# Cross attention with folded weights: another order of the opening work on one NeuronCore

## The chip, the cores and the metric

The program runs on one core of one Trainium2 chip. The metric is the device time of one execution in microseconds (us). The kernel before took 1906.45 us, the median of 3 runs (1904.95 to 1910.61).

## What is computed

The model has two layers of three blocks each. The change touches only the first block of the first layer, a cross attention from 4 x 256 tokens of width 256 to a context of 4096 tokens, with a mask and a single head of width 1024:

```python
x = x + _L0_xattn_ref(_layernorm(x), ctx_1024, ctx_1024, mask, Wq, bq, Wk, bk, Wv, bv, Wo, bo)
...
Q = q @ Wq.T + bq
K = k @ Wk.T + bk
V = v @ Wv.T + bv
e = jnp.einsum('bsd,btd->bst', Q, K) / jnp.sqrt(jnp.float32(d_k))
e = jnp.where(mask == 0, MASK_FILL, e)
a = jax.nn.softmax(e, axis=-1)
y = jnp.einsum('bst,btd->bsd', a, V)
return y @ Wo.T + bo
```

Behind it come a selective scan, a soft mixture of experts, a 16-head cross attention to the same context, a causal attention and a quantised MLP. They are the same in both kernels.

## The kernel before

The block (`cross_attention_wide`, lines 163 to 573) never forms Q, K or V. It folds the weights: A = Wq'Wk (256 x 256) and M = Wv'Wo, so that a score is a token times A times a context column. The biases leave three small things: the column `cq` (Wk'bq, added to the folded queries), the column `u` (Wq'bk, times a token it gives one number of a row) and the number `beta` (bq.bk). From `u` and `beta` comes `small`, and from that `fill`, the value that a masked score gets in each of the 8 query tiles of 128 tokens.

The context arrives transposed, batch by batch (4 batches, two query tiles each), in 8 chunks of 512 columns, 512 KB each. Each chunk is split into two fp32r words: the high word is a cast (line 450, on VectorE, written DVE), the low word is the difference (line 557, on GpSimd, written POOL). A product of two such pairs takes three matmuls per 128 rows (line 156). Both words of every chunk are also stored to memory as `ctx_words` for the second layer, 1 MB per chunk in two transfers (line 220), which SyncE (SP) issues.

The queries are folded in two halves of 512 tokens (line 347), copied out of PSUM by ScalarE (ACT) with `cq` added (line 422) and split into words by VectorE (lines 530 and 532). Then come the tiles. For tile i ScalarE fills a row of scores with the value for masked ones (line 430); TensorE (PE) makes the scores of 8 chunks; VectorE copies the unmasked ones over the filled row (line 458; it counts `kept`) and takes peaks (line 460). ScalarE forms the exponentials in 4 pieces (line 396). In the next turn TensorE transposes them (line 290) and multiplies by the untransposed context, called rows (line 324), while the scores of the tile after are already made. `weighted(i)` is that second part; in it, for each even tile, VectorE also splits the chunks of the next batch. M and the constant row `rowC` (lines 269, 371, 545, 548) are made between the scores of tile 0 and those of tile 1, and tile 1's fill waits for `rowC`.

No planner sets the order. Each engine has one function (`wide_sp`, `wide_pe`, `wide_act`, `wide_dve`, `wide_pool`) and runs it from top to bottom; semaphores tie them together. SP's function is the order in which the transfers enter the queue. Its loop issues the mask of tile i+1 (line 224, 2 MB, one buffer) once tile i's scores are all kept, and around an odd tile the first four chunks of the next batch:

```python
        if i + 1 < NT:
            sp.wait_ge(s.kept, CH * (i + 1))
            load_mask(i + 1)
```

The next batch's chunks use four buffers, so chunks 4 to 7 are loaded one by one behind the stores of chunks 0 to 3. VectorE may overwrite the words of a batch only when all its stores have landed (`split_high` waits for `stored`).

The four weights share memory with the scores: Wq and Wk lie in the scores' first buffer, Wv and Wo in the second.

Of the kernel before, what the change touches and what calls it, by code (L numbers as in the profile page):

```python
# [9 lines left out]
I32 = mybir.dt.int32  # L10
# [151 lines left out]
XW_DH, XW_MASKED, XW_PIECES, XW_RAW = 1024, -2.0 ** 15, 4, 4  # L162
XW_HK = XW_DH // P
# [3 lines left out]
def wide_tiles(k, scope):  # L167
    def sb(name, shape, dt=F32):
# [12 lines left out]
    t["mask"], t["E"] = sb("mask", [P, S2], I32), sb("scores", [P, 2, S2])  # L181
    t["wq"], t["wk"], t["wv"], t["wo"] = (
        t["E"][:, n // 2, n % 2 * HK * D:(n % 2 + 1) * HK * D].rearrange("p (k d) -> p k d", k=HK) for n in range(4))
# [20 lines left out]
def wide_sp(k, t, s, ctxT_in, ctxN_in):  # L204
# [21 lines left out]
    for n in ("Wq", "Wk"):  # L226
        sp.dma_start(t["w" + n[1]], d["L0_xattn_" + n].rearrange("(k p) d -> p k d", p=P)).then_inc(s.wqk, 16)
    load_mask(0)
    for c in range(CH):
        load_words(0, c)  # L230
    for n, name in (("wv", "L0_xattn_Wv"), ("wo", "L0_xattn_WoT")):
        sp.dma_start(t[n], d[name].rearrange("(k p) d -> p k d", p=P)).then_inc(s.wvo, 16)
    for c in range(CH):
        store_words(0, c)
        load_rows(0, c)
    for i in range(NT):
        b = i // QT
# [11 lines left out]
        if i == 0:  # L249
            continue  # L250
# [12 lines left out]
def wide_pe(k, t, s, ctxT_in, ctxN_in):  # L263
    pe, PS, HK = k.pe, k.PS, XW_HK

    def folded(left, right):
        for c in range(KD):
            for h in range(HK):
                last = pe.matmul(PS[:, 4, c * D:(c + 1) * D], left[:, h, c * P:(c + 1) * P], right[:, h, :],
                                 start=(h == 0), stop=(h == HK - 1))  # L270
        return last
# [56 lines left out]
    yt_pe(k, 0, 0)  # L328
    pe.wait_ge(s.wqk, 32)
    folded(t["wq"], t["wk"]).then_inc(s.a_pe, 1)  # L330
    pe.wait_ge(s.biases, 48)
    pe.wait_ge(s.bias_dot, 2)
    for c in range(KD):
        for col, left, right in ((c, t["wk"], t["bq"]), (KD + c, t["wq"], t["bk"])):
            for h in range(HK):
                pe.matmul(PS[:, 5, col:col + 1], left[:, h, c * P:(c + 1) * P], right[:, h:h + 1],
                          start=(h == 0), stop=(h == HK - 1))
    pe.matmul(PS[:, 5, 4:5], k.ones[:], t["dot"][:], start=True, stop=True).then_inc(s.vec_pe, 1)

    pe.wait_ge(s.a, 1)  # L340
    for half in range(TOK // BANK):
        wait_yt(k, pe, 0, half + 1)
        for c in range(KD):
            if half:
                pe.wait_ge(s.q_raw, KD * (half - 1) + c + 1)
            for kd in range(KD):
                last = pe.matmul(PS[:, 6 + c, :], t["A"][:, kd, c * P:(c + 1) * P],
                                 k.YT[:, kd, half * BANK:(half + 1) * BANK], start=(kd == 0), stop=(kd == KD - 1))
            last.then_inc(s.q_pe, 1)
    pe.wait_ge(s.vec, 1)  # L350
# [6 lines left out]
    pe.wait_ge(s.q_lo, 4)  # L357
    for i in range(NT):
        for c in range(CH):
# [3 lines left out]
        if i:  # L363
            weighted(i - 1)
            continue
        pe.wait_ge(s.wvo, 32)
        folded(t["wv"], t["wo"]).then_inc(s.m_pe, 1)
# [13 lines left out]
def wide_act(k, t, s, ctxT_in, ctxN_in):  # L381
# [34 lines left out]
    act.wait_ge(s.vec, 1)  # L416
    for half in range(TOK // BANK):
        for c in range(KD):
            act.wait_ge(s.q_pe, KD * half + c + 1)
            if half:  # L420
                act.wait_ge(s.q_lo, KD * (half - 1) + c + 1)
            act.activation(t["q_raw"][:, c, :], PS[:, 6 + c, :], ACT.Identity, bias=t["cq"][:, c:c + 1],
                           scale=XW_SCALE).then_inc(s.q_raw, 1)
    act.wait_ge(s.small, 2)
    for i in range(NT):
        if i == 1:
            act.wait_ge(s.row, 1)
        if i >= 2:
            act.wait_ge(s.turned, CH * (i - 1))
        act.activation(t["E"][:, i % 2, :], k.zero[:, 0:1].to_broadcast([P, S2]), ACT.Identity,  # L430
                       bias=t["fill"][:, i:i + 1]).then_inc(s.filled, 1)
# [10 lines left out]
def wide_dve(k, t, s, ctxT_in, ctxN_in):  # L442
# [8 lines left out]

    def scores(i):
        dve.wait_ge(s.filled, i + 1)
# [2807 lines left out]
```

## Time and profile before

| | us |
|---|---|
| median of 3 runs | 1906.45 |
| lowest, highest | 1904.95, 1910.61 |
| the profiled execution's own time | 1893.33 |
| its span in the profile | 1891.5 |
| PE busy in it | 1751.8 (93%) |
| DVE busy in it | 1453.6 (77%) |
| ACT busy in it | 1164.5 (62%) |
| mean granted TensorE clock, share of full | 0.969 |

Times in the rows are microseconds from the span's start. L450 is line 450 of the kernel before. "PE" is TensorE's matmuls, "DVE" VectorE, "ACT" ScalarE, "POOL" GpSimd, "SPq" SyncE's issuing of transfers. A matmul of float32 operands shows as two records, so that 16 matmuls stand as x32. The names `xw_scores` on lines 269 and 336 stand for the weights, which lie in that buffer.

### The profile page before, as it was taken

The page shows a single profiled execution, that of the slowest core. Times are in us where ns is not written, and L with a number is a line of the kernel's source. Part 1 is how long each engine was busy: PE and PEld are TensorE (multiplying, and loading weights), DVE is VectorE, ACT ScalarE, POOL GpSimd, SP SyncE. Part 2 cuts the span into 40 slices and gives each one's busy share as a digit, 9 for nine tenths or more (in the row PEclk, how much of TensorE's full clock was granted, in tenths as well). Part 3 has the DMA queues.
Part 4 walks back from the last instruction along what each step waited for, and adds up shares of the span by engine and source line. Part 5 has one row for each costly group of instructions (what it writes and reads, how often), then busy time and mean ns, then how long its engine had stood idle before and what let it go on. Part 6 is the DMA issues. An engine that isn't in the chain of part 4 may idle for free. (4 is left out here: it accounts for less than half of the span.)

```text
span 1891.5 us, 32678 instructions
## 1 busy us (share of the span) xinstructions
PE 1751.8 (93%) x12516; PEld 1202.2 (64%) x12516; DVE 1453.6 (77%) x1664; ACT 1164.5 (62%) x2100; POOL 398.9 (21%) x267
## 2 busy tenths in 40 slices
PE   6989989989999998999988999999999999999875
PEld 5877877457766776878776555555555555555534
DVE  7546643577899886676764899999999999998565
ACT  0333332577777765353541588888888988888363
POOL 4134120145445532232212000010010000000041
PEclk8999999999999999999998899999999999999897
DMA  9798780248866881222225746655566555630000
GB/s 357 271 349 324 276 315 0 95 141 299 317 244 238 304 286 46 69 73 70 73 37 113 173 95 118 123 107 112 103 119 118 107 97 120 116 66 20 1 0 22
DMA packets 171816, 279.79 MB, mean 148 GB/s; under 512 B 21855, under 2 KB 100479, under 8 KB 164495
## 3 DMA queue, kind: packets, MB, share of 16 engines
q1 hardware_dynamic: 170366, 277.52, 51.6%
q8 instruction: 101, 1.65, 0.4%
q10 hardware_dynamic: 1296, 0.19, 0.1%
q14 instruction: 53, 0.43, 0.1%
HBM read 187.07 MB, written 88.14 MB: 146 GB/s over the span
## 5 line engine op out<-in xcount | busy, mean ns | idle before, releaser
L2414 DVE TENSOR_REDUCE xn_peaks<-psum 128x2 f32<-128x1024 f32 x512 | 622.4, 1224 | 41.6 <-PE psum L2212 33.5
L2369 ACT ACTIVATE moe_mix_transposed<-psum 128x512 f32<-128x512 f32 x1024 | 552.6, 597 | 67.6 <-PE psum L2217 34.1
L2217 PE MATMUL psum<-xn_q_stack,xn_k_words 50*128 50x256 f32 x2048 | 374.9, 305 | 6.5 <-DVE xn_peaks L2414 4.0
L2217 PEld LDWEIGHTS psum<-xn_q_stack,xn_k_words 50*128 50x128 f32 x2048 | 248.1, 185 | 206.1 <-ACT moe_mix_transposed L2369 183.4
L2212 PE MATMUL psum<-xn_k_words,xn_q_stack 50*128 50x512 f32 x1024 | 372.4, 452 | 4.6 <-DMA xn_q_stack<-q_rows 3.1
L2249 PE MATMUL psum<-moe_mix_transposed,xn_v 128*32 128x256 f32 x4096 | 327.0, 391 | 2.0 <-issue 0.3
L934 POOL TENSOR_TENSOR mx_state<-mx_du,mx_b_all_channels 128x1024 f32<-128x1024 f32 x64 | 154.0, 2406 | 196.3 <-ACT mx_b_all_channels L1116 83.7
L2212 PEld LDWEIGHTS psum<-xn_k_words,xn_q_stack 50*128 50x128 f32 x1024 | 185.2, 186 | 13.6 <-issue 8.2
L1197 DVE TENSOR_TENSOR_SCAN mx_state<-psum,mx_state 128x1024 f32<-128x1024 f32 x64 | 146.2, 2285 | 50.3 <-ACT psum L1126 42.7
L324 PE MATMUL psum<-xw_ctx_natural,xw_weights_transposed 128*128 128x256 f32 x512 | 124.1, 388 | 12.3 <-DVE xw_weights_transposed L476 12.0
L2249 PEld LDWEIGHTS psum<-moe_mix_transposed,xn_v 128*32 128x32 f32 x4096 | 81.6, 108 | 73.8 <-issue 7.3
L2042 POOL CAST xn_neg_words<-xn_neg_max 128x4 fp32r<-128x4 f32 x32 | 6.1, 190 | 548.3 <-DVE xn_neg_max L2421 548.3
L731 ACT ACTIVATE ctx_k_words<-psum,ctx_bk 128x512 fp32r<-128x512 f32 x128 | 85.5, 690 | 53.5 <-PE psum L156 47.6
L156 PE MATMUL psum<-ctx_wv_words,ctx_chunk_words 128*128 128x256 f32 x768 | 114.6, 299 | 0.6 <-ACT ctx_k_words L731 0.3
L156 PEld LDWEIGHTS psum<-ctx_wv_words,ctx_chunk_words 128*128 128x128 f32 x768 | 101.5, 192 | 17.0 <-issue 12.2
L324 PEld LDWEIGHTS psum<-xw_ctx_natural,xw_weights_transposed 128*128 128x128 f32 x512 | 94.6, 193 | 26.9 <-DVE xw_weights_transposed L476 15.4
L156 PE MATMUL psum<-ctx_chunk_words,ctx_wk_words 128*128 128x512 f32 x384 | 108.0, 423 | 1.5 <-DMA ctx_chunk_words<-ctx_words 1.1
L156 PE MATMUL psum<-moe_w_words,moe_hidden_words 128*128 128x256 f32 x768 | 101.7, 292 | 5.2 <-issue 5.2
L156 PE MATMUL psum<-xw_ctx_transposed_words,xw_q_folded_words 128*128 128x512 f32 x384 | 99.2, 413 | 5.6 <-DVE xw_scores L458 5.0
L156 PE MATMUL psum<-moe_slot_input_words,moe_w_words 128*128 128x512 f32 x384 | 92.7, 395 | 10.7 <-ACT moe_hidden L1581 8.9
L156 PEld LDWEIGHTS psum<-moe_w_words,moe_hidden_words 128*128 128x128 f32 x768 | 95.9, 195 | 9.7 <-issue 8.9
L1206 DVE TENSOR_TENSOR mx_state<-mx_state,mx_c_all_channels 128x1024 f32<-128x1024 f32 x64 | 97.2, 1519 | 0.0
(354 smaller groups left out, 2573.8 us busy)
## 6 DMA issues: line engine op xcount, KB each, us to landing
xn_k_words<-k_words SPq DMA_DIRECT2D x384, 128.0 KB, 6.6
ctx_words<-xw_ctx_transposed_words SPq DMA_DIRECT2D x64, 512.0 KB
ctx_chunk_words<-ctx_words SPq DMA_DIRECT2D x64, 512.0 KB, 5.5
k_words<-ctx_k_words SPq DMA_DIRECT2D x128, 256.0 KB, 2.5
v_all<-ctx_v SPq DMA_DIRECT2D x32, 544.0 KB, 3.2
xn_v<-v_all SPq DMA_DIRECT2D x32, 544.0 KB, 5.1
xw_mask<-in_mask_BxSxS_ik SPq DMA_DIRECT2D x8, 2048.0 KB, 8.2
xw_ctx_natural<-in_ctx SPq DMA_DIRECT2D x32, 512.0 KB, 6.8
```

The costliest lines, as they stand in the source:

```text
L156: last = k.pe.matmul(out, l, r, start=(n == 0), stop=(n == len(terms) - 1))
L324: last = pe.matmul(PS[:, 5, 0:D], t["ET"][:, c % 2, j, :], t["ctxN"][:, c, j, :], start=(c + j == 0), stop=(c == CH - 1 and j == JC - 1))
L731: act.activation(t["keys"][:, m, n, :], k.PS[:, bank("keys", i, m), :], ACT.Identity, bias=t["bk"][:, m:m + 1]).then_inc(kr[m], 1)
L934: pool.tensor_tensor(t["state"][:, i % MX_STATES, :, :], t["du"][:, m % 2, None, :].to_broadcast([P, MX_NQ, MX_HALF]), t["Bb"][:, q * MX_N ...
L1197: dve.tensor_tensor_scan(flat, t["decay"][i % MX_DECAYS].rearrange("p n t -> p (n t)"), flat, 0.0, ALU.mult, ALU.add).then_inc(s.scan, 1)
L1206: dve.tensor_tensor(h, h, t["Cb"][:, q * MX_NQ:(q + 1) * MX_NQ, :], ALU.mult).then_inc(s.cmul, 1)
L2042: pool.tensor_copy(t["neg_words"][:, :, :, XN_SHIFT], neg).then_inc(s.words, 1)
L2212: return pe.matmul(PS[:, 2 * (x % 2) + a, :], Q[narrow_rows(a), m // XN_PAIRS % 2, m % XN_PAIRS, q * P:(q + 1) * P], K[m % XN_KSLOTS][narr ...
L2217: return pe.matmul(PS[:, narrow_bank("exp", n, step, a), half * S:(half + 1) * S], K[n % XN_KSLOTS][narrow_rows(a), kt * P:(kt + 1) * P], ...
L2249: last = pe.matmul(PS[W * j:W * (j + 1), XN_ACC, 0:S], t["V"][:, n % 2, at:at + W], t["weights"][:, step % 4, a, half, :], start=(step == ...
L2369: act.activation(t["weights"][:, step % 4, a, :, :], bank.rearrange("p (t s) -> p t s", t=2), ACT.Exp, scale=XN_SCALE).then_inc(s.taken, 1)
L2414: dve.tensor_reduce(t["peaks"][:, m % 2, q, :, c], PS[:, 2 * (x % 2):2 * (x % 2) + 2, :], AX.X, ALU.max).then_inc(s.top_read, 1)
```

## The change

It changes the opening of the block on each engine.

- The bias `bk` is copied into a 257th column of Wk's tile, so that the fold that makes A gives `u` as its 257th column. `cq` is made as a row, bq'Wk (8 matmuls with a single stationary column and 256 moving ones, into one partition), copied to memory and turned into a column by two matmuls against a one. The 33 matmuls with one moving column of lines 336 and 338 become 2 + 1.
- Batch 0's high words are made by ScalarE (`first_high`), its low words by VectorE (`first_low`). Six high words come ahead of the first half of the queries and two behind; the low words are spread over VectorE's opening. GpSimd has no part in batch 0's words.
- The second half of the queries moves behind the scores of tile 0, on TensorE, ScalarE and VectorE.
- The fills of tiles 0 and 1 are cut into 4 pieces of 1024, and each chunk of scores waits for its own piece.
- `bvB` (8 instructions on VectorE) moves from the opening to behind tile 0's scores.
- SP loads Wk ahead of Wq, the words of batch 0 ahead of the first mask, all rows of batch 0 behind Wv and Wo with no stores between them, and tile 1's mask ahead of the stores. The 16 stores of batch 0 stand behind that mask, and so ahead of batch 1's first chunks.

The core of the diff:

```diff
-    for n in ("Wq", "Wk"):
-        sp.dma_start(t["w" + n[1]], d["L0_xattn_" + n].rearrange("(k p) d -> p k d", p=P)).then_inc(s.wqk, 16)
-    load_mask(0)
+    for n in ("Wk", "Wq"):
+        sp.dma_start(t["w" + n[1]][:, :, 0:D], d["L0_xattn_" + n].rearrange("(k p) d -> p k d", p=P)).then_inc(s.wqk, 16)
     for c in range(CH):
         load_words(0, c)
+    load_mask(0)
...
     for c in range(CH):
-        store_words(0, c)
+        sp.wait_ge(s.ctx_hi, c + 1)
+        sp.wait_ge(s.ctx_lo, c + 1)
         load_rows(0, c)
...
                 if b == 0:
                     sp.wait_ge(s.small, 1)
+                    sp.wait_ge(s.q_pe, 2 * KD)
...
             load_mask(i + 1)
         if i == 0:
+            for c in range(CH):
+                store_words(0, c)
             continue
```

```diff
@@ wide_pe
+    for h in range(HK):
+        last = pe.matmul(PS[0:1, 0, 0:D], t["bq"][:, h:h + 1], t["wk"][:, h, 0:D], start=(h == 0), stop=(h == HK - 1))
+    last.then_inc(s.vec_pe, 1)
+    pe.wait_ge(s.bias_dot, 1)
+    folded(t["wq"], t["wk"], [PS[:, 4 + c, 0:D + 1] for c in range(KD)]).then_inc(s.a_pe, 1)
...
     for c in range(KD):
-        for col, left, right in ((c, t["wk"], t["bq"]), (KD + c, t["wq"], t["bk"])):
-            for h in range(HK):
-                pe.matmul(PS[:, 5, col:col + 1], left[:, h, c * P:(c + 1) * P], right[:, h:h + 1],
-                          start=(h == 0), stop=(h == HK - 1))
+        pe.matmul(PS[:, 1, c:c + 1], t["z"][0:1, c * P:(c + 1) * P], k.ones[0:1, 0:1], start=True, stop=True)
...
     pe.wait_ge(s.a, 1)
+    queries(0)
+    pe.wait_ge(s.vec, 2)
     for q in range(NT):
...
-    pe.wait_ge(s.q_lo, 4)
+    pe.wait_ge(s.q_lo, KD)
...
+        queries(1)
         pe.wait_ge(s.wvo, 32)
```

```diff
@@ wide_act
+    for c in range(XW_SOON):
+        first_high(c)
+    act.wait_ge(s.vec, 2)
+    queries(0)
+    for c in range(XW_SOON, CH):
+        first_high(c)
...
+        pieces = XW_PIECES if i < XW_BY_PIECES else 1
+        for piece in range(pieces):
...
+        if i == 0:
+            queries(1)
@@ wide_dve
+    dve.tensor_copy(t["wk"][:, :, D], t["bk"][:]).then_inc(s.bias_dot, 1)
...
-    for c in range(CH):
-        split_high(0, c)
...
+    first_low(0)
+    first_low(1)
...
+    dve.tensor_copy(t["z"][0:1, :], PS[0:1, 0, 0:D]).then_inc(s.vec, 1)
+    for c in range(2, XW_SOON - 1):
+        first_low(c)
@@ wide_pool
-    for c in range(CH):
-        split_low(0, c)
```

The order of SP's transfers at the block's opening, before (`xw_ctx_natural<-in_ctxT` are batch 0's words, `<-in_ctx` the rows, `ctx_words` the stores; the pair of stores and rows comes eight times, two of them shown):

```order
L224 DMA xw_mask<-in_mask_BxSxS_ik 128x4096
L208 DMA xw_ctx_natural<-in_ctxT 128x2x512 x8
L232 DMA xw_scores<-in_L_xattn_Wv 128x8x256
L232 DMA xw_scores<-in_L_xattn_WoT 128x8x256
L220 DMA ctx_words<-xw_ctx_transposed_words 128x2x512 x2
L212 DMA xw_ctx_natural<-in_ctx 128x4x256
```

and of the change:

```order
L211 DMA xw_ctx_natural<-in_ctxT 128x2x512 x8
L227 DMA xw_mask<-in_mask_BxSxS_ik 128x4096
L235 DMA xw_scores<-in_L_xattn_Wv 128x8x256
L235 DMA xw_scores<-in_L_xattn_WoT 128x8x256
L215 DMA xw_ctx_natural<-in_ctx 128x4x256 x8
L227 DMA xw_mask<-in_mask_BxSxS_ik 128x4096
L223 DMA ctx_words<-xw_ctx_transposed_words 128x2x512 x16
L211 DMA y_normed<-in_ctxT 128x2x512 x2
L211 DMA y_transposed<-in_ctxT 128x2x512 x2
L227 DMA xw_mask<-in_mask_BxSxS_ik 128x4096
```

The 16 stores of batch 0 now stand between tile 1's mask and batch 1's first four chunks; from tile 2's mask on the order is the old one.

VectorE's opening before, from the copy of A on:

```order
L518 COPY xw_a<-psum 128x512
L450 CAST xw_ctx_transposed_words<-xw_ctx_natural 128x1024 x8
L522 TENSOR_SCALAR xw_cq<-psum 128x2
L523 COPY xw_u<-psum 128x2
L524 COPY xw_bq_dot_bk<-psum 128x1
L530 CAST xw_q_folded_words<-xw_q_folded 128x512
L532 TENSOR_TENSOR xw_q_folded_words<-xw_q_folded,xw_q_folded_words 128x512
```

and of the change, from the small bias products on:

```order
L485 TENSOR_TENSOR xw_ctx_transposed_words<-xw_ctx_natural,xw_ctx_transposed_words 128x1024 x2
L567 COPY xw_z<-psum 1x256
L485 TENSOR_TENSOR xw_ctx_transposed_words<-xw_ctx_natural,xw_ctx_transposed_words 128x1024 x3
L571 COPY xw_a<-psum 128x512
L572 COPY xw_u<-psum 128x2
L574 TENSOR_SCALAR xw_cq<-psum 128x2
L575 COPY xw_bq_dot_bk<-psum 128x1
L485 TENSOR_TENSOR xw_ctx_transposed_words<-xw_ctx_natural,xw_ctx_transposed_words 128x1024
L493 CAST xw_q_folded_words<-xw_q_folded 128x512
```

The eight casts that stood between A and `cq` are gone; five low words now lie ahead of A, in VectorE's wait for the fold, and one behind `cq`.

## Rows read from the trace of the kernel before

**Rows 1.** The page's busy line, and the chain of waits asked for 0 to 130 us

```profile
PE 1751.8 (93%) x12516; PEld 1202.2 (64%) x12516; DVE 1453.6 (77%) x1664; ACT 1164.5 (62%) x2100; POOL 398.9 (21%) x267
0 pieces in order of time: start us, us, what
```

**Rows 2.** Timeline of TensorE, 14 to 76 us: start, duration, what, [idle before it]

```profile
14.85 7.59 PE L269 MATMUL psum<-xw_scores 128*128 128x256 f32 x32
28.86 3.55 PE L336 MATMUL psum<-xw_bk,xw_scores 128*128 128x1 f32 x16
...
32.70 5.50 PE L347 MATMUL psum<-y_transposed,xw_a 128*128 128x512 f32 x8
...
47.15 4.20 PE L353 MATMUL psum<-xw_u,y_transposed 128*128 128x1 f32 x32
51.21 13.96 PE L156 MATMUL psum<-xw_ctx_transposed_words,xw_q_folded_words 128*128 128x512 f32 x48
65.00 7.07 PE L269 MATMUL psum<-xw_scores 128*128 128x256 f32 x32
71.91 3.62 PE L371 MATMUL psum<-xw_scores,xw_bv_all_columns 128*128 128x256 f32 x16
```

**Rows 3.** Timeline of VectorE, 22 to 56 us

```profile
22.48 0.69 DVE L518 COPY xw_a<-psum 128x512 f32<-128x512 f32 x1 [5.70 <-PE psum L269]
23.09 17.79 DVE L450 CAST xw_ctx_transposed_words<-xw_ctx_natural 128x1024 fp32r<-128x1024 f32 x8
40.80 0.15 DVE L522 TENSOR_SCALAR xw_cq<-psum 128x2 f32<-128x2 f32 x1
...
43.40 2.72 DVE L532 TENSOR_TENSOR xw_q_folded_words<-xw_q_folded,xw_q_folded_words 128x512 fp32r<-128x512 f32 x1
...
46.48 0.69 DVE L532 TENSOR_TENSOR xw_q_folded_words<-xw_q_folded,xw_q_folded_words 128x512 fp32r<-128x512 f32 x1
...
55.59 0.73 DVE L458 COPY_PREDICATED xw_scores<-xw_mask,psum 128x512 f32<-128x512 int32 x1 [3.77 <-ACT xw_scores L430]
```

**Rows 4.** Timeline of ScalarE, 41 to 56 us

```profile
41.11 1.26 ACT L422 ACTIVATE xw_q_folded<-psum,xw_cq 128x512 f32<-128x512 f32 x2 [25.43 <-DVE xw_bq_dot_bk L524]
...
51.85 3.71 ACT L430 ACTIVATE xw_scores<-zero,xw_fill 128x4096 f32<-128x4096 f32 x1 [3.81 <-DVE xw_fill L537]
```

**Rows 5.** Issues of 3 to 4 and of 6.6 to 6.8 us: KB, us to landing

```profile
xw_mask<-in_mask_BxSxS_ik SPq DMA_DIRECT2D x1, 2048.0 KB, 15.9
...
xw_ctx_natural<-in_ctxT SPq DMA_DIRECT2D x1, 512.0 KB, 13.9
```

**Rows 6.** Busy time by stretch: PE, PEld, DVE, ACT, POOL, granted clock, DMA share, GB/s

```profile
20.00:26.00 6.00, 6.00 (x47) 5.72 (x45) 3.52 (x4) 0.00 (x0) 2.08 (x1) 1.00 1.05 388
26.00:32.00 6.00, 6.00 (x31) 6.00 (x31) 6.00 (x3) 0.00 (x0) 6.00 (x3) 0.51 1.07 366
...
50.00:57.00 7.00, 7.00 (x21) 5.76 (x22) 1.77 (x5) 4.99 (x2) 0.00 (x0) 0.51 1.06 400
57.00:65.00 8.00, 8.00 (x36) 6.47 (x35) 7.79 (x13) 0.00 (x0) 0.00 (x0) 1.00 1.06 399
...
79.00:90.00 11.00, 10.94 (x52) 8.64 (x51) 9.98 (x15) 1.33 (x2) 2.67 (x4) 1.00 0.00 0
```

**Rows 7.** Timeline of SP's issuing, 65 to 110 us

```profile
65.97 0.35 SPq L224 DMA_DIRECT2D xw_mask<-in_mask_BxSxS_ik  x1
...
90.12 0.34 SPq L224 DMA_DIRECT2D xw_mask<-in_mask_BxSxS_ik  x1
94.95 0.88 SPq L220 DMA_DIRECT2D ctx_words<-xw_ctx_transposed_words  x2
...
107.50 1.51 SPq L208 DMA_DIRECT2D y_transposed<-in_ctxT  x1
```

**Rows 8.** Timeline of VectorE, 102 to 178 us, its splits of batches 1 and 2

```profile
102.64 0.75 DVE L450 CAST xw_ctx_transposed_words<-y_normed 128x1024 fp32r<-128x1024 f32 x1 [3.68 <-DMA ctx_words<-xw_ctx_transposed_words]
...
114.69 0.69 DVE L450 CAST xw_ctx_transposed_words<-y_transposed 128x1024 fp32r<-128x1024 f32 x1 [3.33 <-DMA ctx_words<-xw_ctx_transposed_words]
...
178.31 0.69 DVE L450 CAST xw_ctx_transposed_words<-y_transposed 128x1024 fp32r<-128x1024 f32 x1 [3.06 <-DMA y_transposed<-in_ctxT]
```

**Rows 9.** Busy time of 156 to 158 us, columns as in rows 6

```profile
156.00:158.00 2.00, 2.00 (x13) 1.74 (x13) 1.93 (x4) 0.00 (x0) 0.00 (x0) 1.00 0.00 0
```

More of the change, by code:

```diff
@@ L264, in wide_pe, with folded, queries @@
     pe, PS, HK = k.pe, k.PS, XW_HK
-    def folded(left, right):
-        for c in range(KD):
-            for h in range(HK):
-                last = pe.matmul(PS[:, 4, c * D:(c + 1) * D], left[:, h, c * P:(c + 1) * P], right[:, h, :],
-                                 start=(h == 0), stop=(h == HK - 1))
-        return last
+    def folded(left, right, outs):
+        for c, out in enumerate(outs):
+            for h in range(HK):
+                last = pe.matmul(out, left[:, h, c * P:(c + 1) * P], right[:, h, :], start=(h == 0), stop=(h == HK - 1))
+        return last
+    def queries(half):
+        wait_yt(k, pe, 0, half + 1)
+        for c in range(KD):
+            if half:
+                pe.wait_ge(s.q_raw, KD * (half - 1) + c + 1)
+            for kd in range(KD):
+                last = pe.matmul(PS[:, 6 + c, :], t["A"][:, kd, c * P:(c + 1) * P],
+                                 k.YT[:, kd, half * BANK:(half + 1) * BANK], start=(kd == 0), stop=(kd == KD - 1))
+            last.then_inc(s.q_pe, 1)
     def scores(i, c):
@@ L365, in wide_pe @@
             continue
+        queries(1)
         pe.wait_ge(s.wvo, 32)
-        folded(t["wv"], t["wo"]).then_inc(s.m_pe, 1)
+        folded(t["wv"], t["wo"], [PS[:, 4, c * D:(c + 1) * D] for c in range(KD)]).then_inc(s.m_pe, 1)
         pe.wait_ge(s.small, 1)
@@ L415, in wide_act, with first_high, queries @@
     yt_act(k, 0)
-    act.wait_ge(s.vec, 1)
-    for half in range(TOK // BANK):
+    def first_high(c):
+        act.wait_ge(ctxT_in[c], 16)
+        act.copy(t["ctxT"][:, c, 0, :, :], t["raw"](0, c)).then_inc(s.ctx_hi, 1)
+    def queries(half):
         for c in range(KD):
@@ L429, in wide_act @@
             act.wait_ge(s.turned, CH * (i - 1))
-        act.activation(t["E"][:, i % 2, :], k.zero[:, 0:1].to_broadcast([P, S2]), ACT.Identity,
-                       bias=t["fill"][:, i:i + 1]).then_inc(s.filled, 1)
+        pieces = XW_PIECES if i < XW_BY_PIECES else 1
+        for piece in range(pieces):
+            width = S2 // pieces
+            act.activation(t["E"][:, i % 2, piece * width:(piece + 1) * width], k.zero[:, 0:1].to_broadcast([P, width]),
+                           ACT.Identity, bias=t["fill"][:, i:i + 1]).then_inc(s.filled, 1)
+        if i == 0:
+            queries(1)
         if i:
@@ L537, in wide_dve @@
     dve.tensor_scalar(t["fill"][:], t["small"][:], XW_MASKED, None, ALU.add).then_inc(s.small, 1)
+    for c in range(XW_SOON + 1, CH):
+        first_low(c)
     for i in range(NT):
@@ L543, in wide_dve @@
         row_peak(0)
+        queries(1)
+        for h in range(HK):
+            last = dve.tensor_scalar(t["bvB"][:, h, :], k.ones[:], t["bv"][:, h:h + 1], None, ALU.mult)
+        last.then_inc(s.wide, 1)
         dve.wait_ge(s.m_pe, 1)
```

80 lines of the change are left out of this document (42 added, 38 removed).

## The prediction

> **What bounds the kernel now.** The busy line puts TensorE at 93% of the span, but that is an average over six blocks, and the chain of waits says nothing of this one: asked for the first 130 us it has no piece there [rows 1]. So I read the first 180 us engine by engine in the timelines, and then the transfers.
>
> TensorE first [rows 2]: fold of A until 22.4, bias products until 32.4, first half of the queries until 38.2, then a wait for the queries to be copied out, the `u` products from 47.15, and tile 0's scores only from 51.2. Who held it back is VectorE [rows 3]: between A (ready at 23.2) and `cq` (40.8) stand eight casts of context words, 17.8 us of them, and ScalarE waited 25.4 us for `cq` and its two neighbours [rows 4]. Then ScalarE fills a whole row, 3.7 us, before VectorE keeps its first score at 55.6 [rows 3, 4]. When the last chunk is kept, SP issues tile 1's mask: that is the mark of tile 0's end, 65.97 [rows 7]. Tile 1's end is the next mask, at 90.12.
>
> Behind that the bound is another one. From 90 on VectorE waits for transfers at each split, and splits batch 1's last chunk at 114.69 [rows 8]. Tile 2's scores need it. The transfer engines had nothing to do from 79 to 90 [rows 6], then 8 MB in a row: tile 2's mask (2), stores of chunks 0 to 3 (4), chunks 4 to 7 (2). The last of these is issued at 107.50 [rows 7]. So whatever is gained in front counts only as far as that last chunk lands earlier.
>
> **The change, part by part.** Times are those of the profiled execution (its own time 1893.33, which is 13.1 us under the median of the runs; I take the difference of the kernels from the trace and put it on the median).
>
> *Biases and A.* On TensorE bq'Wk comes ahead of the fold: 8 matmuls of 256 columns, 16 records at 7.59/32 = 0.24 us, 3.8 us [rows 2]. No row has a matmul with one stationary column; the bounds are 1.9 us (half, if it ran as a shorter one) and 7.6 us (at half clock), and I take 3.8, since the moving side is that of line 269. The fold starts at 18.7 in place of 14.85 and ends near 26.5; its 257th column is 16 columns more in 4096, below 0.1 us. VectorE copies A (0.7), `u`, `cq`, `beta` (0.15 each), with three small matmuls between: `cq` is there at about 27.9 instead of 41.0. The low words that precede it lie in VectorE's wait for the fold. Cover gone: if words come late. Batch 0's first chunk was issued at 6.7 and landed at 20.6, behind a mask of 2 MB that landed at 19.3 [rows 5]; with that mask behind the words it comes about 2.1 MB / 0.39 = 5.4 us earlier, near 15.4, the next ones 1.3 us apart. ScalarE casts each in about 1.0 us (a quarter of the 3.7 of a row of 4096 [rows 4], though that reads a constant; between 0.9 and 1.3), VectorE subtracts in 1.2 us (twice 0.69 less the fixed part [rows 3]). Five are done by about 24, 2.5 us ahead of the fold.
>
> *GpSimd left out.* The same subtraction took 2.72 us beside GpSimd and 0.69 without it [rows 3]. VectorE's opening now has 8 x 1.2 us without a neighbour where it had 17.8. This is inside the 13 us above, not on top.
>
> *Queries.* The first half takes 5.5 us in a stretch where the granted clock was about 0.5 after the one-column products (26 to 32 us: 0.51, the lower of its two levels, 1.2 GHz [rows 6]). These products are gone, so I take full clock, 3.4 us, with 5.5 as the other end. It runs from 27.5 to 31; the copy and split of it (0.7 + 0.4 + 0.7, twice, staggered) end by 33 behind the `u` products. Those start at 31 and take 4.2 us [rows 2]: TensorE is ready for tile 0 at 35.2, where it was at 51.2. The second half no longer stands in front; it follows tile 0's scores.
>
> *Tile 0.* From the end of the `u` products to the next mask the old kernel took 65.97 - 51.21 = 14.8 us. The clock falls in it as before (0.51 from 50 to 57, behind the `u` products [rows 6]), so I keep this duration. The fill in pieces lets VectorE begin about 2 us sooner than 4.4 us behind TensorE, but TensorE at half clock is then what it waits for: worth 0.3 us, at most 1. Tile 1's mask is issued at 35.2 + 14.5 = 49.7, **16.3 us earlier**. The first mask, now behind the words, lands near 30, seven us before its first use: nothing. Wv and Wo, and the rows, go through the queue with no stores between and are there by 45: nothing.
>
> *Tile 1.* From TensorE's end of tile 0 (48.7): second half 3.6 (3.4 and a start), M 7.1, row 3.6 [rows 2], constant row 0.5, one piece of the fill 1.0, then 10.4 for eight chunks (55.59 to 65.97 [rows 3, 7]): kept by 74.9 where it was 90.1, **15.2 us earlier**. ScalarE's exponentials wait for the second half of the queries, some 5 us later against tile 0's scores; they end near 60, before the fill that waits for the row at 64. VectorE's `bvB` lies in its wait for M: nothing.
>
> *The stores.* 16 transfers, 8 MB, leave the opening, where the queue ran on beside the engines' work, and go behind tile 1's mask. What stands behind them in SP's queue are batch 1's chunks 0 to 3, and behind these tile 2's mask. From 49.7 on the queue must carry 12 MB (mask 2, stores 8, chunks 2) and then the same 8 MB as before, for which the old kernel took 114.69 - 90.12 = 24.6 us. 12 MB are 12.6 million bytes, at the 399 to 400 GB/s of the mixed stretch from 50 to 65 us [rows 6] 31.5 us. Sum: 49.7 + 31.5 + 24.6 = 105.8 for the split that stood at 114.69. VectorE's own path (15.2 us earlier) is ahead of that, and tile 2's mask (issued about 75) is in the queue before the chunks have drained at 81, so no hole opens. The gain is **8.9 us**, and 15.2 - 8.9 = 6.3 us of what was won in front turn into VectorE's waits for transfers between 75 and 106.
>
> On the path that sets the end: the rate of these 20 MB. A rule speaks against the rate that I use. The Trainium skill, DMA: Bandwidth & Descriptors, Specifications, gives a limit of about 358 GB/s between HBM and one core; the trace does not agree, with 400 GB/s over 7 us [rows 6]. By that limit the 20 MB would take 58.6 us in place of 52.4, an estimate that would cut the gain to 2.7.
>
> *Behind it.* Before batch 2 the queue is empty again (156 to 158: 0 GB/s [rows 9]), and its splits wait for transfers as those of batch 1 did, e.g. at 178.31 [rows 8]. That pattern starts from the tiles, so the shift is carried to the block's end and through the five blocks behind, whose code is the same.
>
> So 1893.3 - 8.9 = 1884.4 for a profiled execution, and 1906.45 - 8.9 = **1897.5** for the median. A difference under 0.3% (5.7 us) can't be told from none here.
>
> **Rivals.**
> - *The transfers don't bind (gain 15.2, 1891.3).* The old wait at 102.64 could be one for stores of batch 1 or its order alone. Then the last chunk would have to land at 99.5: 21.0 million bytes in 49.8 us, 421 GB/s with no time to start or to land. Against it stand 400 GB/s with the engines' share above 1 [rows 6]. Chance 0.12.
> - *The long run of transfers is slower (gain 4.0, 1902.5).* Eight MB of stores without loads between is a mix that no row shows. The slowest full stretch in the rows is 366 GB/s, from 26 to 32 us, when stores had joined the loads [rows 6]; at that rate 20 MB take 57.3 us in place of 52.4, and the gain is 8.9 - 4.9. Against it: stores and loads together ran at 400 from 50 to 57. Chance 0.07. The Trainium skill's limit, named above, would send the kernel this way.
> - *The front wins less (gain 1 to 5, about 1903).* If TensorE's clock falls on bq'Wk, the fold takes up to 7.6 us longer, and 8.9 shrinks to 1.3; if the words come 2.6 us later than worked out, the low words delay A by as much. For: the clock did fall after the one-column products [rows 2, 6]. Against: those stream one column per load, these 256, as line 269 does at clock 1.00. Chance 0.12.
> - *Slower, by the stores' new place.* 12 MB now lie between tile 0's end and tile 2's mask; the old kernel had 24.2 us there, and they need 31.5. Where tile 0 ends less than 7.4 us earlier, batch 1's last chunk lands later than before; with a front that wins nothing the time is 1906.45 + 7.4 = 1913.9. It decides at 7.4 us, and I expect 16.3. For it only the price is sure. Chance 0.06, with what makes it more than 5.7 us slower under half of that; the rest of the slower side is a waiting order on SP that I have not seen.
>
> **How the numbers follow.** Forecast 0.63, rivals 0.12, 0.07, 0.12, 0.06. The predicted time is that of the forecast, 1897.5; its own bounds are 1894 (rate 415 GB/s, or a front 2 us better) and 1902 (half clock for the queries and 385 GB/s). Down to 1889 the range takes in the first rival with 2 to 3 us of scatter, up to 1907 the third. Faster by over 0.3% means a gain of 5.7 or more: most of the forecast (0.60 of 0.63) and the first rival, and a part of the third, 0.76; within 0.3% 0.18; slower 0.06.
>
> **What would show it.** The eight casts gone from between A and `cq`; `cq` near 28; TensorE's tile 0 from 35; SP's second mask near 50, the third near 76; transfers without a gap from 50 to about 106 at 395 to 405 GB/s; VectorE's last split of batch 1 near 106, with waits for transfers of some 6 us more in all than before; from there to the end the same distances. I am wrong if the last split of batch 1 shifts by another amount than the end of the span, if the granted clock is 0.5 in the fold, or if the transfers of 50 to 80 us run below 380 GB/s.

## The result, and the profile after

| | before | after |
|---|---|---|
| median of the first 3 runs, us | 1906.45 | 1889.98 |
| lowest, highest | 1904.95, 1910.61 | 1888.43, 1891.06 |
| the profiled execution's own time | 1893.33 | 1889.98 |
| its span | 1891.5 | 1888.1 |
| mean granted clock | 0.969 | 0.970 |

The recorded ratio of these runs is 0.9895 (95% interval 0.9849 to 0.9941); the two medians by themselves give 0.9914, 16.5 us, where 8.9 were forecast. The profiled execution of the kernel before was not one of its three timed runs, that of the change was, and the two profiled spans differ by 3.4 us. So the first question is how much the change is worth at all; two further timings of the unedited change (e1 and e12 below) put it at 7.2 us, and the profile says where they come from. Means, intervals and counts below leave out as slow three executions more than 1.5% above the fastest of their kernel: 1920.9 and 1923.4 of the kernel before, and 1909.5 of e5.

The timeline of TensorE after the change, from 14 to 63 us, answers to [rows 2] (start, duration, what):

```profile
14.84 4.06 PE L349 MATMUL psum<-xw_scores,xw_bq 128*1 128x256 f32 x16
18.83 7.22 PE L276 MATMUL psum<-xw_scores 128*128 128x257 f32 x32
...
26.84 3.70 PE L285 MATMUL psum<-y_transposed,xw_a 128*128 128x512 f32 x8
30.38 4.57 PE L365 MATMUL psum<-xw_u,y_transposed 128*128 128x1 f32 x32
34.81 13.64 PE L156 MATMUL psum<-xw_ctx_transposed_words,xw_q_folded_words 128*128 128x512 f32 x48
48.29 3.60 PE L285 MATMUL psum<-y_transposed,xw_a 128*128 128x512 f32 x8
51.72 7.07 PE L276 MATMUL psum<-xw_scores 128*128 128x256 f32 x32
58.63 3.62 PE L386 MATMUL psum<-xw_scores,xw_bv_all_columns 128*128 128x256 f32 x16
```

The row of bq'Wk takes 4.1 us, the fold ends at 26.05, the first half of the queries runs at full clock (3.7 us, no longer 5.5), and tile 0 begins at 34.8 in place of 51.2.

VectorE's timeline, which answers to [rows 3] and, in its last line, to [rows 8]:

```profile
16.51 2.36 DVE L485 TENSOR_TENSOR xw_ctx_transposed_words<-xw_ctx_natural,xw_ctx_transposed_words 128x1024 fp32r<-128x1024 f32 x2 [1.38 <-ACT xw_ctx_transposed_words L434]
...
19.28 3.47 DVE L485 TENSOR_TENSOR xw_ctx_transposed_words<-xw_ctx_natural,xw_ctx_transposed_words 128x1024 fp32r<-128x1024 f32 x3
26.10 0.69 DVE L571 COPY xw_a<-psum 128x512 f32<-128x512 f32 x1 [3.34 <-PE psum L276]
...
26.94 0.16 DVE L574 TENSOR_SCALAR xw_cq<-psum 128x2 f32<-128x2 f32 x1
...
81.66 0.69 DVE L481 CAST xw_ctx_transposed_words<-y_normed 128x1024 fp32r<-128x1024 f32 x1 [4.81 <-DMA y_normed<-in_ctxT]
...
107.84 0.69 DVE L481 CAST xw_ctx_transposed_words<-y_transposed 128x1024 fp32r<-128x1024 f32 x1 [3.46 <-DMA y_transposed<-in_ctxT]
```

Two low words take 2.36 us; VectorE still waits 3.3 us for the fold, so they cost nothing. `cq` stands at 26.94, 13.9 us earlier. Then the picture turns: the first split of batch 1 waits 4.8 us for its chunk, and the last one is at 107.84, where it was at 114.69. That is 6.85 us gained of 16.65 at tile 1's mask, which SP's timeline shows ([rows 7]):

```profile
49.32 0.34 SPq L227 DMA_DIRECT2D xw_mask<-in_mask_BxSxS_ik  x1
49.75 20.43 SPq L223 DMA_DIRECT2D ctx_words<-xw_ctx_transposed_words  x16
70.27 2.59 SPq L211 DMA_DIRECT2D y_normed<-in_ctxT  x2
...
75.99 1.70 SPq L227 DMA_DIRECT2D xw_mask<-in_mask_BxSxS_ik  x1
```

What the transfer engines did, from busy time by stretch (PE, PEld, DVE, ACT, POOL, granted clock, DMA share, GB/s), answers to [rows 6]:

```profile
42.00:44.00 2.00, 2.00 (x10) 1.64 (x9) 1.93 (x4) 0.00 (x0) 0.00 (x0) 1.00 1.10 348
44.00:47.00 3.00, 3.00 (x15) 2.40 (x14) 2.93 (x5) 0.00 (x0) 0.00 (x0) 1.00 0.82 263
47.00:49.00 2.00, 2.00 (x9) 1.40 (x8) 1.97 (x4) 0.00 (x0) 0.00 (x0) 1.00 0.03 9
49.00:50.00 1.00, 1.00 (x3) 0.38 (x2) 0.96 (x2) 0.00 (x0) 0.00 (x0) 1.00 0.00 0
50.00:55.00 5.00, 5.00 (x21) 3.65 (x20) 3.61 (x13) 3.73 (x5) 0.00 (x0) 1.00 1.01 338
55.00:60.00 5.00, 5.00 (x25) 4.41 (x24) 1.06 (x3) 3.56 (x8) 0.00 (x0) 1.00 0.92 328
60.00:65.00 5.00, 4.44 (x20) 3.44 (x19) 0.83 (x2) 2.26 (x3) 2.14 (x4) 1.00 1.05 407
65.00:70.00 5.00, 5.00 (x23) 4.04 (x22) 4.86 (x8) 2.01 (x2) 3.48 (x5) 1.00 1.05 404
```

They stand still from 47 to 50, then work until the last split without standing still again. The new hole in front and the closed one at 79 to 90 are the same thing: work that was hidden beside the opening has become a stream behind tile 0.

### The profile page after: what moved, and what is told of

Read it like the earlier page. It is cut to its first block and busy times, and to the rows that moved or that the text cites. A ratio compares the mean times of both kernels' runs of the same rounds, so it can differ in the third digit from the quotient of the medians.

```text
span 1888.1 us, 32668 instructions
## 1 busy us (share of the span) xinstructions
PE 1746.3 (92%) x12472; PEld 1195.3 (63%) x12472; DVE 1442.5 (76%) x1666; ACT 1173.5 (62%) x2114; POOL 377.9 (20%) x259
```

## The experiments

Each was timed in turn with the kernel before on one chip: e1, e3, e4 and e5 on the first, e6 to e9 on the second, e10 to e12 on the third. "Last split" is VectorE's split of batch 1's chunk 7 in the profiled execution, "mask" SP's issue of tile 1's mask.

| kernel | ratio to before | 95% interval | mask | last split |
|---|---|---|---|---|
| before | | | 65.97 | 114.69 |
| the change, first profile | 0.9895 | 0.9849 to 0.9941 | 49.32 | 107.84 |
| e1, the change | 0.9955 | 0.9936 to 0.9975 | 45.37 | 104.00 |
| e12, the change | 0.9976 | 0.9948 to 1.0004 | 49.18 | 106.51 |
| e4, only the stores moved | 1.0066 | 1.0034 to 1.0099 | 65.89 | 124.17 |
| e3, stores back | 0.9968 | 0.9945 to 0.9991 | 58.78 | 108.43 |
| e5, half the stores first | 0.9930 | 0.9905 to 0.9955 | 48.98 | 101.86 |
| e10, the same | 0.9953 | 0.9923 to 0.9983 | 49.80 | 102.72 |
| e11, the same with u as a row | 0.9947 | 0.9921 to 0.9972 | 48.93 | 101.72 |
| e6, low words by GpSimd | 0.9967 | 0.9940 to 0.9994 | 46.74 | 104.44 |
| e7, one-column products | 1.0015 | 0.9985 to 1.0045 | 57.51 | 115.84 |
| e8, fills in one piece | 0.9970 | 0.9946 to 0.9994 | 49.44 | 106.48 |
| e9, queries together | 0.9981 | 0.9958 to 1.0005 | 50.72 | 108.72 |

**The change again, twice (e1, e12).** No edit.

> The changed kernel itself, timed in turn with the kernel before on one chip. The two profiled spans differ by 3.4 us (1891.5 and 1888.1), the medians of the first runs by 16.5. Theory A: the traces are right, and the first three runs of the kernel before were all some 12 us long for a reason that has nothing to do with the code (its own profiled execution took 1893.3): paired, the change is 3 to 8 us faster, ratio 0.996 to 0.998. Theory B: 16 us are a real gain that the profiled execution of the kernel before did not show: ratio near 0.991. In the trace both expect tile 1's mask issued at 49.3 and the last split of batch 1 at 107 to 109.

> The changed kernel once more, for the size of its gain: with the first comparison (ratio 0.9955) the theory that the traced shift of the last split is the gain (7 us and more, depending on the clock behind the u products) expects 0.995 to 0.997. If the first three runs (16.5 us) were the truth, 0.991.

On the first chip the means are 1894.6 us (12 executions) and, of the kernel before, 1903.3 (35), on the third 1898.4 (12) and 1904.1 (27): gains of 8.8 and 5.6, 7.2 us in the mean with a standard error of about 1.4. e12 by itself could still be no gain: its interval reaches 1.0004. The size is that of Theory A, but its reason is not borne out. The kernel before ranges from 1890.9 to 1916.7 over its 93 executions beside the experiments, on three chips, with a mean of 1904.0. Its first three (mean 1907.3) lie only 3.3 us above that, and 33 of the 93 took as long as the shortest of them or longer. What was unusual is its profiled execution, 1893.3: only one of the 93 was shorter. And the first three of the change (mean 1889.8) lie 6.7 us below the mean of its 24 executions in e1 and e12, 1896.5, of which only five took 1891.06 or less. So three runs that agree within 3 to 6 us may still all lie on one side, and most of what the first figures had too much came from the side of the changed kernel.

Part of what makes that range is visible. Over the 93 executions the mean granted clock (0.956 to 0.972) and the time have a correlation of -0.87. In the profiles, the part of the program where they differ most is the second layer's 16-head attention, far behind the change. Stretches of 100 us there, first of the kernel before, then of e5, then two of e4:

```profile
1370.00:1470.00 100.00, 98.18 (x1058) 56.22 (x1053) 91.65 (x84) 84.22 (x167) 7.03 (x13) 1.00 0.66 121
```

```profile
1370.00:1470.00 100.00, 99.11 (x946) 55.41 (x943) 82.44 (x76) 75.35 (x149) 6.66 (x11) 0.86 0.57 105
```

```profile
1370.00:1470.00 100.00, 99.05 (x1013) 56.49 (x1009) 87.98 (x79) 81.14 (x162) 6.66 (x11) 0.94 0.57 106
1470.00:1570.00 100.00, 99.80 (x1043) 54.99 (x1040) 89.99 (x78) 83.41 (x161) 2.28 (x9) 0.92 0.54 98
```

The clock falls for a while in code that is the same in all three, and where it does fewer matmuls fit into 100 us (946 for 1058). From the first to the last matmul of line 2249 it is 664 us in the profiles of before, after and e1, 675 in that of e5, 682 in e12 and 683 in e4 (the line's number in the other kernels differs). Hence the spans of single profiles can't be subtracted to some us, but the places of the opening can, and they are what I compare below.

Even the opening has such a choice in it. TensorE in e1 (timeline):

```profile
29.57 3.63 PE L365 MATMUL psum<-xw_u,y_transposed 128*128 128x1 f32 x32
33.06 11.45 PE L156 MATMUL psum<-xw_ctx_transposed_words,xw_q_folded_words 128*128 128x512 f32 x48
```

The same instructions took 4.57 and 13.64 in the first profile. By stretch, the first profile, then e1:

```profile
36.00:38.00 2.00, 2.00 (x7) 1.52 (x6) 0.69 (x2) 2.00 (x3) 0.00 (x0) 0.50 1.11 349
```

```profile
36.00:38.00 2.00, 2.00 (x10) 1.64 (x9) 1.97 (x4) 1.97 (x2) 0.00 (x0) 1.00 1.10 347
```

Behind the one-column `u` products the granted clock fell to its lower level (1.2 GHz) in the first profile and did not in e1. Tile 1's mask is 4.0 us apart: 0.9 of them are in the products, 2.2 in tile 0, and the rest arose before, since e1 began its products at 29.57 for 30.38. It did not fall in e6 either; in e12, e3, e5, e10 and e8 it did.

**Only the stores moved (e4).** Kernel before, with

```diff
     for c in range(CH):
-        store_words(0, c)
+        sp.wait_ge(s.ctx_hi, c + 1)
+        sp.wait_ge(s.ctx_lo, c + 1)
         load_rows(0, c)
...
         if i == 0:
+            for c in range(CH):
+                store_words(0, c)
             continue
```

> The kernel before with nothing but the stores of batch 0 moved behind tile 1's mask. By the sum of the prediction the last split of batch 1 goes from 114.7 to 65.97 + 56 to 58.5 = 122 to 124.5, 7.4 to 10 us later, and the span grows by as much or a little less: ratio 1.003 to 1.005. A rival (the place of the stores costs nothing, the transfers ahead of the splits are not what is waited for): no change, ratio within 0.001 of 1.

The mask stays at 65.89, the last split goes to 124.17, 9.5 us later, and the time is 0.66% longer, 12.6 us. So this part of the change is a loss by itself, and the rival that puts it on the slower side has its price measured, if by one profile: it decides where tile 0 ends less than 9.5 us earlier, not 7.4. The two effects add up to within 1 us. What a kernel gains at the mask, less 9.5, gives 7.2 us at the last split for the change, 11.1 for e1 and 7.3 for e12; measured are 6.9, 10.7 and 8.2.

**Stores back (e3).** The change without that part:

```diff
     for c in range(CH):
-        sp.wait_ge(s.ctx_hi, c + 1)
-        sp.wait_ge(s.ctx_lo, c + 1)
+        store_words(0, c)
         load_rows(0, c)
...
         if i == 0:
-            for c in range(CH):
-                store_words(0, c)
             continue
```

> The change, but with each chunk's stores of batch 0 ahead of its rows, where the kernel before had them. Theory A (the queue's idle time is what is lost: it stood still from about 42 to 49 us and everything behind 49 is one long stream of 20 MB): the stores fill that hole, tile 1's mask lands near 66 instead of 57 and delays tile 1 by some 4 us, but the last split of batch 1 comes near 105, about 3 us earlier than the change's 107.8. Theory B (the stores' new place is part of the gain): the last split comes later than 107.8, since tile 1's mask waits behind 8 MB of stores, 111 or more.

Neither cleanly: Theory B's reason, but not its amount. The last split is at 108.43, 0.6 us behind the change's. The hole is filled, but SP issued tile 1's mask only at 58.78: it was still handing stores to a full queue, and a mask that was due at 49 stood behind them. What the stream lost in length came back as a late tile 1 (tile 2's mask at 83.89 instead of 75.99). From that mask to the last split it is 24.5 us, as in the kernel before (24.6).

**Half the stores first (e5, and again e10).** The change with

```diff
         load_rows(0, c)
+    for c in range(CH // 2):
+        store_words(0, c)
     for i in range(NT):
...
-            for c in range(CH):
+            for c in range(CH // 2, CH):
                 store_words(0, c)
```

> The change, with the stores of chunks 0 to 3 ahead of tile 1's mask and those of 4 to 7 behind it. The queue has 7 us of nothing ahead of 49.3 in the changed kernel. If the length of the stream behind it sets the last split of batch 1, 4 MB of stores go into the hole for the most part: mask landed near 59 to 60, still ahead of tile 1's first use at 63, last split near 102, and the end 4 to 6 us earlier than the change. If the stream is not what binds: no difference to the change.

> The kernel with four chunks' stores ahead of tile 1's mask once more, beside the change on the same chip. By the traces its last split comes 6 us before the change's where both have the fallen clock behind the u products (101.9 and 107.8). So 3 to 6 us faster than the change in this comparison, ratio 0.992 to 0.994 against the kernel before. If the stores' place made no difference outside the profiled executions: the change's ratio.

The mask goes out as early as with all stores behind it (48.98 and 49.80), and the last split is at 101.86 and 102.72, where the change had it at 107.84 and, in e12, at 106.51: 3.8 to 6.0 us earlier, all four with the fallen clock. The engines' stretch that was 338 GB/s in the change (50 to 55) is full here:

```profile
45.00:50.00 5.00, 5.00 (x19) 3.31 (x18) 4.73 (x8) 0.13 (x1) 0.00 (x0) 1.00 1.07 393
50.00:55.00 5.00, 5.00 (x21) 3.77 (x20) 3.78 (x12) 3.94 (x6) 0.00 (x0) 1.00 1.05 408
```

In time, the mean of this kernel is 3.9 us under the change's on the first chip (1890.7 and 1894.6; 2.4 if the execution of 1909.5 is counted) and 3.7 on the third (1894.8 and 1898.4). Each has an error of some 2 to 3 us by itself, both together about 1.9. It clearly beats the kernel before, by 12.7 and 9.3 us; that it beats the change too is likely, by two differences that agree and by the places in the trace, and not sure.

**One-column products (e7).** The change with line 336's products back:

```diff
-    for h in range(HK):
-        last = pe.matmul(PS[0:1, 0, 0:D], t["bq"][:, h:h + 1], t["wk"][:, h, 0:D], start=(h == 0), stop=(h == HK - 1))
-    folded(t["wq"], t["wk"], [PS[:, 4 + c, 0:D + 1] for c in range(KD)]).then_inc(s.a_pe, 1)
+    folded(t["wq"], t["wk"][:, :, 0:D], [PS[:, 4 + c, 0:D] for c in range(KD)]).then_inc(s.a_pe, 1)
...
+        for col, left, right in ((c, t["wk"], t["bq"]), (KD + c, t["wq"], t["bk"])):
+            for h in range(HK):
+                pe.matmul(PS[:, 1, col:col + 1], left[:, h, c * P:(c + 1) * P], right[:, h:h + 1],
+                          start=(h == 0), stop=(h == HK - 1))
```

> The change, but with the 33 one-column bias products behind the fold as before, in place of the row of bq'Wk and the 257th column. Theory A (they are worth their own 10.5 us and the clock that falls with them, less the 4 us of the row): cq near 33, queries at half clock, tile 1's mask near 57, 7 to 8 us later than the change, and the end as much later. Theory B (the words' transfers hold the opening anyway): mask by 52 and the end within 3 us of the change.

Theory A. TensorE's timeline:

```profile
22.49 1.84 PE L353 MATMUL psum<-xw_bq,xw_scores 128*128 128x1 f32 x16
...
28.48 3.55 PE L353 MATMUL psum<-xw_bk,xw_scores 128*128 128x1 f32 x16
31.89 0.56 PE L355 MATMUL psum<-xw_bq_dot_bk_partial,ones 128*128 128x1 f32 x2
32.32 6.11 PE L285 MATMUL psum<-y_transposed,xw_a 128*128 128x512 f32 x8
```

The last 16 records of the products take 3.55 us for the first 16's 1.84, and the queries 6.1 us for 3.7. The mask is 8.2 us later, the last split 8.0, and with it the whole gain is gone: 1.0015, no difference to the kernel before. What is left of the change still brings the mask 8.5 us forward (57.51 for 65.97), and the stores' new place takes that back: 8.5 less e4's 9.5 puts the last split 1.0 us behind that of the kernel before, and it came 1.15 behind. So the row and the 257th column are needed for the gain. That they would be worth little alone is argued and not tried: in the kernel before, the products ended near 32.8, and the eight casts held `cq` until 40.80. No run takes those casts away by themselves either.

**Low words by GpSimd (e6).** GpSimd runs `split_low(0, c)` for all eight, VectorE none; TensorE waits for the second half of the transposed tokens ahead of `u`.

```diff
-    first_low(0)
-    first_low(1)
...
+    for c in range(CH):
+        split_low(0, c)
     k.pool.wait_ge(s.row, 1)
```

> The change, but batch 0's low words are made by GpSimd again (the high words stay with ScalarE); TensorE waits for both halves of the transposed tokens ahead of the u products, which are long there. Theory A (only two engines on one port cost something): the split of the queries on VectorE goes from 1.1 to some 4 us for each half column beside GpSimd, tile 1's mask is issued 2 to 4 us later than with the change, at 49 to 53 (45 to 49 with the clock at full behind the u products), and the last split of batch 1 by as much. Theory B (VectorE's free opening hides it, GpSimd's 2.4 us per chunk end in time): no shift of the mask over 1 us.

Neither cleanly, nearer to B. The clock stayed at full, so e1 is the one to compare: mask 1.4 us later (of which 0.7 is a later start of tile 0), last split 0.4 later. Two of VectorE's instructions grew beside GpSimd. A cast of the queries, from 0.43 to 1.48, had 1 us to spare. The instruction that makes `fill`, from 0.17 to 0.87, had none: ScalarE's fill waits for it and VectorE's first copy for ScalarE, 1.27 us, and from there VectorE takes its eight chunks at the pace of e1. That is the other 0.7 us at the mask.

```profile
29.54 1.48 DVE L489 CAST xw_q_folded_words<-xw_q_folded 128x512 fp32r<-128x512 f32 x1 [2.49 <-ACT xw_q_folded L442]
31.05 0.69 DVE L491 TENSOR_TENSOR xw_q_folded_words<-xw_q_folded,xw_q_folded_words 128x512 fp32r<-128x512 f32 x1
...
34.19 0.87 DVE L572 TENSOR_SCALAR xw_fill<-xw_small 128x8 f32<-128x8 f32 x1
36.34 0.77 DVE L503 COPY_PREDICATED xw_scores<-xw_mask,psum 128x512 f32<-128x512 int32 x1 [1.27 <-ACT xw_scores L460]
```

So sparing GpSimd is worth 0.7 us here, little beside the 16.65 at the mask.

**Fills in one piece (e8).** One number: `XW_BY_PIECES` 0 in place of 2.

> The change with the fills of tiles 0 and 1 in one instruction each. Theory A (the stream of transfers binds behind tile 0, and in tile 0 TensorE is late anyway): tile 1's mask 0 to 1.5 us later, tile 2's mask some 3 us later but still ahead of the drained queue, last split of batch 1 and the end 0 to 1.5 us later. Theory B (VectorE's path binds): end 3 to 5 us later.

Theory A: the mask is 0.1 us later, tile 2's mask 1.0 us later (76.98), and the last split even 1.4 us earlier, no more than the change's own two profiles with the fallen clock differ by (107.84 and 106.51). The pieces are worth nothing that shows here.

**Queries together (e9).** `queries(1)` directly behind `queries(0)` on all three engines.

> The change with the second half of the queries back in front of tile 0, on all three engines. Theory A: tile 0 begins 3.6 to 5 us later, and so does the stream of transfers behind tile 1's mask (mask at 53 to 54.5, or 49 to 50.5 with the clock at full), though tile 1 begins at the same time; last split and end 3.6 to 5 us later. Theory B (what counts is when tile 1 begins): no shift of the end.

The time is in the direction of A, though its interval overlaps the change's; the places less so: tile 0 begins at 36.54, 1.7 us after the first profile's 34.81 and 3.5 after e1's; the mask is 1.4 and 5.4 us later; the last split 0.9 and 4.7. Of the five microseconds against e1 1.6 are the clock (tile 0 took 13.00 us for 11.45), which in e9 fell at 38 us. Theory B is out in the trace: tile 1's scores begin at 60.47, 2.3 us ahead of the first profile's 62.81, and yet the last split is 0.9 behind. How much of A is true, one profile doesn't say.

**u as a row (e11).** e5 with

```diff
-    for q in range(NT):
-        for kd in range(KD):
-            last = pe.matmul(PS[:, 5, q:q + 1], k.YT[:, kd, q * P:(q + 1) * P], t["u"][:, kd:kd + 1],
+    for half in range(2):
+        for kd in range(KD):
+            last = pe.matmul(PS[0:1, 3 + half, :], t["u"][:, kd:kd + 1], k.YT[:, kd, half * BANK:(half + 1) * BANK],
...
+            last = pe.matmul(PS[:, 5, q:q + 1], t["ET"][0:1, half, j, :], k.ones[0:1, 0:1], start=True, stop=True)
```

> The last kernel, with the 16 one-column u products in place of which come 4 matmuls with u as the stationary column over all tokens (a row), a copy of the row by ScalarE, and 8 small ones that turn it into columns. If the one-column products are what the clock falls on: granted clock 1.00 through tile 0, TensorE's tile 0 begins about 1 us later (near 36) but takes 11.5 us in place of 13.6, mask near 48, last split 1 us earlier than without, ratio the same within 0.001. Rival: the clock falls for another reason (the pause of the copy, the move to half-busy work), 0.50 in 35 to 42 as before, and the mask comes near 50.5.

TensorE's timeline:

```profile
30.77 3.59 PE L368 MATMUL psum<-y_transposed,xw_u 128*1 128x512 f32 x8
34.29 1.94 PE L375 MATMUL psum<-ones,xw_weights_transposed 1*128 1x1 f32 x16
36.16 11.47 PE L156 MATMUL psum<-xw_ctx_transposed_words,xw_q_folded_words 128*128 128x512 f32 x48
```

As the first theory expected: tile 0 begins at 36.16 and takes 11.47, at a granted clock of 1.00 throughout; mask 48.93, last split 101.72. But e1 and e6 had the full clock with the products in place, so one profile without a fall doesn't show that the row prevents it; that stays open. The time is that of e5.

## Why the prediction was right and wrong

**The opening: right, nearly to the microsecond.** `cq` at 27.9 (measured 27.0), fold until 26.5 (26.05), tile 0 from 35.2 (34.8), tile 1's mask 49.7 (49.32), tile 2's mask 74.9 (75.99). The unknown price of a matmul with one stationary column, 3.8 us taken between 1.9 and 7.6, came out at 4.06 and, over all profiles, between 3.62 and 4.62. Of the 16.65 us at the mask the row and its column account for 8.2 (e7); the rest wasn't taken apart. The queries ran at full clock as chosen. What I took for settled and was not is the fall of the clock behind the `u` products: it comes in some executions only, and is worth about 3 us at the mask.

**The stream: right in kind, 2.0 us too cheap.** The prediction has the last split of batch 1 at 105.8; it came at 107.84, so the trace's gain there is 6.85 and not 8.9. The mask was 0.4 us earlier than said, so the term that was mis-sized is "31.5 + 24.6": 56.1 us from tile 1's mask to the last split. It measured 58.5, 58.6, 57.3 (the change, e1, e12) and 58.3 (e4). I had costed its first 12 MB at the rate of a stretch in full flow, 400 GB/s. But the engines moved nothing until 50, 0.7 us after the mask was issued, and the first 10 us from there ran at 333 (338 and 328 above), with two dips, one when the engines start and one from 56 to 57 (205 GB/s), by their order where the stores follow the mask's load. Ten microseconds at 333 in place of 400 are 1.7 us, an estimate; with the 0.7 that makes the 2.4 us between 58.5 and 56.1. The Trainium skill, DMA: Bandwidth & Descriptors, Specifications, has about 358 GB/s as the limit between HBM and one core, and 21.0 million bytes in 58.5 us come to 358 in the mean. The trace doesn't bear the limit out: the same stream ran at 404 to 407 GB/s from 60 to 75, and the engines moved 381 in the mean of the whole stretch, more than those 20 MB, since SP had issued further stores from 100.57 on:

```profile
49.32:107.84 58.52, 49.56 (x214) 39.97 (x214) 27.32 (x47) 21.99 (x29) 22.60 (x15) 0.91 1.02 381
```

VectorE waited 19.0 us for transfers ahead of the eight splits of batch 1, where it had waited 13.0, the 6 us more that were forecast. Two of the three signs by which the prediction said that it would be wrong came. The last split shifted by 6.85 us and the end of the span by 3.4, and the transfers of 50 to 80 us ran at 373 GB/s, below 380. The third did not: the clock in the fold was 1.00.

**The gain at the end: 7.2 us in 24 executions against 62, and 16.5 in the first three of each, for 8.9 forecast.** The step that failed is one that I thought needed no argument: "I take the difference of the kernels from the trace and put it on the median". It carries the 13.1 us between the profiled execution and the median of the kernel before over to the changed kernel: 1884.4 for a profiled execution, 1897.5 for the median. The changed kernel has no such distance; its profiled execution, 1889.98, is the median of its three. The 13.1 us were chance, from an execution shorter than all but one of 93. With them the noise was put too low: 0.3% as the limit of what can be told, and 2 to 3 us of scatter in the range. The 93 executions have a standard deviation of 5.4 us, so that a difference of two means of three has an error of 4.4 us, and a measurement with three of each can't tell 9 us from 16 or from 3. The means of the first three differ by 17.5 us, a little over two such errors above 7.2; about 3 of the excess is on the side of the kernel before and 7 on that of the change. Beyond the scatter nothing on record explains them, and whether the chip of those runs had a part in it stays open. That 1897.5 lies only 1.0 us from the 1896.5 that the changed kernel takes in the mean of 24 is in part luck: it starts 2.4 us above the mean of the kernel before, 1904.0, and takes off 8.9 where these two means differ by 7.5.

**"The shift is carried to the end": not shown by one profile.** The shift was 7.3 us at tile 3's mask, 5.2 at the block's end and 3.4 at the program's. From the last split to the last score of the block it took 176.3 us in the profile of before and 176.9 to 179.5 in the twelve others. From the block's last statistics to the first multiplication of the scan it was 48.4 in before, 48.8 in e10 and 50.2 to 51.1 in the eleven others, among them e4, whose opening is the old one apart from the stores. Both stretches were at the low end in that one profile of before; the paired times, 7.2 us for shifts of 6.85, 10.7 and 8.2 at the last split, show that most of the shift is not given back.

**The rivals.** "The transfers don't bind" is out: the first split of batch 1 waits 4.8 us for its chunk, and in e5 and e10 the last split comes earlier by nothing but the place of eight stores. "The long run of transfers is slower" had half its amount, 2.4 us for 4.9, but not its reason: the stores ran at 404 to 407 GB/s once they flowed, and the time went at the start. "The front wins less" is out. "Slower, by the stores' new place" is the mechanism of e4, 9.5 us, more than the prediction's 7.4, and the change escapes it only because the opening wins 16.65. GpSimd's part, which I counted inside VectorE's 13 us, is worth 0.7 us of its own (e6). The pieces of the fill, for which I had 0.3 us in tile 0 and 2.7 in tile 1 (a piece of 1.0 for a row of 3.7), gave 0.1 and 1.0 at the two masks and nothing at the last split (e8). The bias products, for which I had only the clock's level, turn out to be the part on which the whole gain hangs (e7).

## What to carry to other kernels

When a kernel's opening is shortened, ask what rode along beside it for nothing: here 8 MB of stores lost their cover and became a stream in front of the next batch, 9.5 us of loss that took more than half of a gain of 16.65. A transfer that nobody waits for belongs into the hole ahead of the urgent one, but only as much of it as the queue has handed on when the urgent one is due; half was better here than either, and all was no better than none. And look at the distance between the profiled execution and the timed ones before any sum: where it is larger than the gain that you are about to predict, three runs of each will not show that gain.

## What the runs showed of the hardware

- The granted clock differs between executions of the same code, for a reason that no run shows. The same instructions behind 16 products of one moving column had 0.50 for six microseconds in one execution and 1.00 in another (the rows above), and it fell at different places of the same 660 us of attention.
- Loads that fill the engines run at different rates. Batch 0's rows (runs of 1 KB) went at 348 GB/s at a share of 1.10, and the loads of 14 to 20 us, by their order its words (runs of 2 KB), at 386 at a share of 1.05. Those of 20 to 26 us, by their order the end of the words and then the mask (runs of 16 KB), went at 422 at a share of 1.08. That the length of the runs is the cause was not tried:

```profile
14.00:20.00 6.00, 6.00 (x26) 2.91 (x25) 4.42 (x8) 4.57 (x5) 0.00 (x0) 1.00 1.05 386
20.00:26.00 6.00, 6.00 (x29) 4.94 (x28) 2.75 (x3) 2.10 (x2) 0.00 (x0) 1.00 1.08 422
```

- A matmul of float32 with a single stationary column and 256 moving ones takes no less time than one with 128 stationary columns: 16 records in 3.62 us in e1 and up to 4.62 in e10, where 16 with 128 stationary columns took 3.62 (line 386), at a granted clock of 1.00 each time. What made some of the former longer stays open.
